# A GNN kernel: stores awaited one block later, row statistics made inside the edge count, and a head's sums taken out by two wide operations

## The reference

```
x = x + _L0_gnn_ref(_layernorm(x, axis=-1), L0_gnn_W_fc, L0_gnn_attn_l, L0_gnn_attn_r, L0_gnn_W_res, src, dst)
x = x + _L0_ffn_ref(_layernorm(x, axis=-1)[None], ...)[0]
x = x + _L1_gnn_ref(_layernorm(x, axis=-1), edge_index, edge_type_3, ...)
x = x + _L1_ffn_ref(_layernorm(x, axis=-1)[None], ...)[0]
```

```
hh = h.reshape(n, H, D)
ft = jnp.einsum('nhd,ed->nhe', hh, W_fc)
a1 = jnp.einsum('nhd,hd->nh', ft, attn_l)
a2 = jnp.einsum('nhd,hd->nh', ft, attn_r)
e = jax.nn.leaky_relu(a1[src] + a2[dst], negative_slope=NEG_SLOPE)
m = jax.ops.segment_max(e, dst, num_segments=n)
ee = jnp.exp(e - m[dst])
denom = jax.ops.segment_sum(ee, dst, num_segments=n)
alpha = ee / denom[dst]
agg = jax.ops.segment_sum(alpha[:, :, None] * ft[src], dst, num_segments=n)
res = jnp.einsum('nhd,ed->nhe', hh, W_res)
return jax.nn.relu((res + agg).reshape(n, H * D))
```

## Time and profile before

| | us |
|---|---|
| median of 3 runs | 3301.93 |
| lowest and highest | 3301.04, 3302.32 |
| the profiled execution's own time | 3298.07 |
| its span, first to last instruction | 3296.3 |
| PE busy | 2732.4 (83%) |
| DVE busy | 2093.9 (64%) |
| ACT busy | 1294.1 (39%) |
| mean granted TensorE clock | 0.891 |

### The profile page before, as it was taken

How to read it: one execution, slowest core, us unless ns; L and a number is a source line. 1 busy time by engine, 2 the same in 40 slices (tenths; PEclk the granted TensorE clock), 3 DMA queues, 4 the chain that set the end, 5 groups by cost and what they waited for, 6 DMA issues and landing times. The chain is left out here.

```text
span 3296.3 us, 35744 instructions
## 1 busy us (share of the span) xinstructions
PE 2732.4 (83%) x12628; PEld 2026.0 (61%) x12629; DVE 2093.9 (64%) x3230; ACT 1294.1 (39%) x1728; POOL 301.7 (9%) x148
## 2 busy tenths in 40 slices
PE   7867966888566966997999997997999599998869
PEld 3546962233236853555999985996888455565544
DVE  6755998999843545982889887506768760124351
ACT  1563217988410001113888872215556310013210
POOL 0000000000045851000000003300000000000002
PEclk9987558999868988998999997998999699999969
DMA  1556526101026545424532313425334310000031
GB/s 65 149 157 156 163 86 250 47 31 47 29 59 213 190 148 197 171 80 139 153 101 82 100 52 134 163 76 174 123 121 145 124 37 29 29 30 1 1 85 47
DMA packets 173005, 344.95 MB, mean 105 GB/s; under 512 B 28821, under 2 KB 94813, under 8 KB 172091
## 3 DMA queue, kind: packets, MB, share of 16 engines
q1 hardware_dynamic: 127924, 253.57, 25.2%
q10 hardware_dynamic: 35968, 73.97, 6.3%
q0 software_dynamic: 8960, 15.41, 1.9%
HBM read 259.93 MB, written 82.91 MB: 104 GB/s over the span
## 5 line engine op out<-in xcount | busy, mean ns | idle before, releaser
L1260 PE MATMUL rg1a_acc<-rg1a_values,rg1a_high 125*125 125x193 f32 x2400 | 407.5, 334 | 40.3 <-DMA rg1a_values<-values_dram 20.2
L1260 PEld LDWEIGHTS rg1a_acc<-rg1a_values,rg1a_high 125*125 125x125 f32 x2400 | 403.0, 192 | 45.0 <-issue 22.6
L1421 PE MATMUL gat_acc<-far_u,gat_ft 125*65 125x512 f32 x720 | 287.4, 540 | 76.2 <-DVE far_u L1485 75.8
L1302 DVE TENSOR_TENSOR rg1a_high<-rg1a_high,rg1a_lowb 125x625 f32<-125x625 f32 x240 | 194.3, 810 | 118.6 <-ACT rg1a_lowb L1278 103.6
L1421 PEld LDWEIGHTS gat_acc<-far_u,gat_ft 125*65 125x65 f32 x720 | 94.3, 142 | 265.6 <-issue 171.0
L1056 PE MATMUL rg_out<-rg_w,rg_hT 128*125 128x384 f32 x720 | 234.3, 489 | 0.0
L1942 PE MATMUL rg2a_acc<-rg2a_value_part,rg2a_wts_part 125*125 125x512 f32 x600 | 206.3, 344 | 28.5 <-DVE rg2a_wts_part L1661 18.9
L1277 ACT ACTIVATE rg1a_high<-rg1a_rows,rg_ks 125x625 f32<-125x625 f32 x240 | 196.3, 818 | 70.2 <-PE rg1a_acc L1260 40.6
L1943 PE MATMUL rg2a_acc<-rg2a_value_part,rg2a_wts_part 125*125 125x512 f32 x600 | 206.8, 345 | 0.0
L1944 PE MATMUL rg2a_acc<-rg2a_value_part,rg2a_wts_part 125*125 125x512 f32 x600 | 205.2, 342 | 0.0
L1056 PEld LDWEIGHTS rg_out<-rg_w,rg_hT 128*125 128x125 f32 x720 | 135.7, 189 | 97.5 <-issue 1.8
(11 more groups left out here) (433 smaller groups left out, 5205.0 us busy)
## 6 DMA issues: line engine op xcount, KB each, us to landing
rg2a_values<-values_dram SPq DMA_DIRECT2D x90, 384.0 KB, 3.3
rg1a_values<-values_dram SPq DMA_DIRECT2D x240, 96.0 KB, 1.9
rg_mask<-far_dram SPq DMA_DIRECT2D x60, 312.5 KB, 3.4
moe_raw<-in_L_ffn_w SPq DMA_DIRECT2D x16, 1152.0 KB, 6.8
gat_rows<-rows_dram SPq DMA_DIRECT2D x12, 1250.0 KB, 5.7
rg1a_rows<-shift_dram SPq DMA_DIRECT2D x24, 625.0 KB, 6.8
relw_chunk<-in_L_gnn_W ACTq DMA_DIRECT2D x36, 384.0 KB, 3.1
sorted_dram<-gat_zeros SPq DMA_DIRECT2D x30, 384.0 KB, 10.9
```

Of the source, the lines that this page charges most:

```text
L1260: last = pe.matmul(tile_of(u, d), wts[i % HB][:, d * TP:(d + 1) * TP], stream[i % 4][:, :], start=first and d % per_bank == 0, stop=final, ...
L1302: dve.tensor_tensor(high[i % HB][:, 0:w], high[i % HB][:, 0:w], lowb[i % LB][:, 0:w], op=ALU.max).then_inc(max_done, 1)
L1421: last = pe.matmul(acc[h % 2][0:WIDTH, b, 0:c1 - c0], ft[:, t, h, :], wts[i % HB][:, c0:c1], start=(t == 0), stop=(t == NT - 1))
```

## The change

Three edits, all in the first layer.

1. SP no longer waits for the stores of `far` and `counts` in the count's block. The buffers and semaphores of these stores move into an object of their own, `CountStores`, at the other end of the on-chip memory. The waits (`wait_all`) are made by SP in the block of the first norm, and the memory is given back after it.
2. The first norm gets `stats=g.row_stats`. The ten row statistics are made by DVE in the count, one tile (two instructions) at the end of the iterations 14, 15, 17, 18, 20, 21, 23, 24, 26 and 27, with one more wait for x ahead of the first. Those are the iterations that have no merge.
3. In `take_out` the ten operations of 64 columns become two of 640. One multiplies the sums in PSUM by the reciprocals (each read 64 times) into a new buffer `shares`, tied by `link`; the other adds it to `res`.

```diff
@@ count_edges
-        far = [sb(f"far{b}", [TP, N], BF16) for b in range(2)]
-        counts = [sb(f"counts{i}", [TP, NT, GROUP], U16) for i in range(2)]
+        far, counts, far_out, counts_out = stores.far, stores.counts, stores.far_out, stores.counts_out
...
             send_counts(KT // 3 - 1)
             sp.wait_ge(x_in, 48)
-            for i in range(2):
-                sp.wait_ge(far_out[i], KT // 2 * 32)
-            for i in range(2):
-                sp.wait_ge(counts_out[i], KT // 6 * 32)
...
                 if k % 3 == 1 and k >= 7:
                     merge(k // 3 - 2)
+                elif k % 3 != 1 and k >= 14:
+
+                    t = (k - 14) - (k - 13) // 3
+                    if t == 0:
+                        dve.wait_ge(x_in, 48)
+                    if t < NT:
+                        last = row_stats(dve, g, g.x, t)
+                        if t == NT - 1:
+                            last.then_inc(stats_done, 1)
             dve.wait_ge(merged, MERGED)
+            dve.wait_ge(stats_done, 1)
@@ new, ahead of count_edges
+class CountStores:
+    def __init__(self, s):
+        self.far = [s.sb(f"far{b}", [TP, N], BF16, side="right") for b in range(2)]
+        self.counts = [s.sb(f"counts{i}", [TP, NT, 3 * TP], U16, side="right") for i in range(2)]
+        self.far_out, self.counts_out = s.sems("far_out", 2), s.sems("counts_out", 2)
+
+    def wait_all(self, sp):
+        for i in range(2):
+            sp.wait_ge(self.far_out[i], KT // 2 * 32)
+        for i in range(2):
+            sp.wait_ge(self.counts_out[i], KT // 6 * 32)
@@ normalize, at the end of SP's part
+            if stored:
+                stored.wait_all(sp)
@@ attend_narrow, take_out
-                for d in range(NT):
-                    at = slice(h * DV, (h + 1) * DV)
-                    last = dve.scalar_tensor_tensor(out=res[:, d, at], in0=by_tile[:, d // HALF, d % HALF, 0:DV],
-                                                    scalar=recip[:, d:d + 1], in1=res[:, d, at],
-                                                    op0=ALU.mult, op1=ALU.add)
-                last.then_inc(taken, 1)
+                link(dve.tensor_tensor(shares[:, :, :].rearrange("p (a d) w -> p a d w", a=2), by_tile[:, :, :, 0:DV],
+                                       recip[:, :].rearrange("p (a d) -> p a d", a=2).unsqueeze(3)
+                                       .to_broadcast([TP, 2, HALF, DV]), op=ALU.mult))
+                at = slice(h * DV, (h + 1) * DV)
+                dve.tensor_tensor(res[:, :, at], res[:, :, at], shares[:, :, :], op=ALU.add).then_inc(taken, 1)
@@ gat_layer
-                normalize(g, "gat_ln", g.x, res, hT)
+                normalize(g, "gat_ln", g.x, res, hT, stats=g.row_stats, stored=stores)
+                stored.close()
```

More of the change, by code:

```diff
@@ L53, in __init__, with sb @@
             g.semaphores_used = 0
-    def sb(self, name, shape, dt=F32):
-        return self.ctx.enter_context(self.nc.sbuf_tensor(name, shape, dt))
+    def sb(self, name, shape, dt=F32, side="left"):
+        return self.ctx.enter_context(self.nc.sbuf_tensor(name, shape, dt, side=side))
     def ps(self, name, shape):
@@ L112, in _, with count_edges @@
             pool.wait_ge(ident_done, 1)
-def count_edges(g, x, src, dst, etype):
+class CountStores:
[8 more added lines that the diff above has]
+            sp.wait_ge(self.counts_out[i], KT // 6 * 32)
+def count_edges(g, x, src, dst, etype, stores):
     with ExitStack() as ctx:
@@ L164, in count_edges @@
         far_done = sem("far_done")
-        far_out = [sem(f"far_out{b}") for b in range(2)]
         turned_done = sem("turned_done")
         turned_copied = sem("turned_copied")
-        counts_out = [sem(f"counts_out{i}") for i in range(2)]
+        stats_done = sem("count_stats_done")
         masks_in = [sem(f"masks_in{i}") for i in range(2)]
@@ L421, in turn_tile, with normalize @@
     last.then_inc(tiled, 1)
-def normalize(g, tag, src, dst, dstT, gamma=None, beta=None, eps=1e-5, beside=None, stats=None):
+def normalize(g, tag, src, dst, dstT, gamma=None, beta=None, eps=1e-5, beside=None, stats=None, stored=None):
     with ExitStack() as ctx:
@@ L1381, in attend_narrow @@
         recip = s.sb(f"{tag}_recip", [TP, NT])
+        shares = s.sb(f"{tag}_shares", [TP, NT, DV])
         acc = [s.ps(f"{tag}_acc{i}", [128, 3, 512]) for i in range(2)]
@@ L1705, in gat_layer @@
     H, DH = 12, 64
-    with ExitStack() as ctx:
-        count_edges(g, x, src, dst, etype)
+    stored = ExitStack()
+    stores = CountStores(Scope(g, stored))
+    count_edges(g, x, src, dst, etype, stores)
     with ExitStack() as ctx:
```

## The result

| | before | after |
|---|---|---|
| median, us | 3302.23 (5 runs) | 3279.46 (5 runs) |
| lowest and highest, us | 3301.04, 3304.97 | 3274.26, 3284.73 |
| the profiled execution's own time, us | 3298.07 | 3279.46 |
| its span, us | 3296.3 | 3277.7 |
| its mean granted TensorE clock | 0.891 | 0.895 |

The ratio of after to before is 0.9933, with a 95% interval of 0.9921 to 0.9945: 22.8 us less by the medians. From profile to profile it is 18.6 us less, where the sum said 17.8. The median lies 0.5 us under the low end of the range of the forecast.

A forecast was written before the change was run, and what follows sets the result against it. No engine was taken to bound the whole; each place was read for the wait that ends last. Terms 4.9 + 9.3 - 0.5 + 4.1 = 17.8 us less gave 3284.1 us against the median of 3301.93, range 3280 to 3293.

The forecast's parts named there:

- The stores' wait: End of the count's block: without SP's wait for the last stores the norm starts earlier, 4.9 us less.
- the rival that its end drains them: Count's block end: leaving it waits for the stores anyway, so the 4.9 us stay; 3289.0 us, chance 5%.
- the last rival: Statistics cost PE their full time and the block's end still waits for stores; 3297.8 us together, chance 2%.
- The statistics in the norm: Start of the first norm: DVE's 20 statistics instructions, alone on the path, go; 9.3 us less.
- The statistics in the count: Count: the same 20 instructions return, 0.93 us a tile at ten places, mostly hidden; 0.5 us more.
- the walk: Count, place by place from timelines: PE feels four of ten delays, by 0.1 to 0.2 us each; 0.5 us more.
- The lower bound of -2 us: Statistics in the count: shifted work could spare two slow PE batches of 1.0 us from clock falls.
- the statistics show in full: Count: each 0.93 us is handed on to PE, costing 9.3 for 0.5; 3292.9 us, chance 13%.
- slower: Count: PE's clock falls at each of the ten places, costing 29.3 us; 3312.9 us, chance 3%.
- The wide operations: Attention, a head's sums: two operations of 640 columns for ten, 0.34 us less a head, 4.1 us for twelve.
- The rival of dear operations: Attention: PSUM pattern and repeated operand make the wide operations dear, bringing only 1.0 us; 3287.2 us, chance 5%.
- What else could move: PE's clock in the norm, up to 0.8 us gain but nothing taken; projection, some 2 us either way allowed.

The follow-up runs named there:

- e1: The kernel before with only the stores' wait moved into the norm's block: median 3295.53 us, ratio to before 0.9993.
- e3: The kernel before with only a head's ten operations made two wide ones: median 3296.43 us, ratio to before 0.9989.
- e2: The kernel before with only the row statistics moved into the count: median 3292.60 us, ratio to before 0.9981.
- e4: The changed kernel, unaltered, timed once more: median 3282.10 us, ratio to before 0.9947.
- e7: The changed kernel with the projection's six weight loads issued by SP in the norm: median 3277.28 us, ratio to before 0.9917.
- e8: The changed kernel with the projection's weights, last two masks and first tile of counts loaded in the norm: median 3272.67 us, ratio to before 0.9908.
- e9: The changed kernel, unaltered, on one chip with e10 and e11: median 3284.13 us, ratio to before 0.9947.
- e10: The changed kernel with weights, two masks and first counts tile loaded in the norm, run again: median 3275.64 us, ratio to before 0.9917.
- e11: As e10, plus 13 unused identity matmuls keeping PE busy in the norm and projection: median 3267.71 us, ratio to before 0.9904.
- e5: The changed kernel with six extra unused statistics instructions at each of the ten places, run once: span 3301.2 us, count's last closing matmul 19.1 us later.
- e6: The changed kernel with the same statistics put behind the count's merges, run once: span 3301.1 us, count's last closing matmul 14.0 us later.

## Why the prediction held, and which terms were off

**The stores' wait: right.** The sum took 4.9 us. The start moved from 5.5 us behind SP's last issue to 0.75, so 4.8 us, in after as in e1. The 0.6 us that I took for the block's end were 0.75. The block can be left with its stores under way; the rival that its end drains them, at 3289.0, is refuted by this row, and with it the last rival, 3297.8. The cover was there too: the wait ends near 237.2 and the projection starts at 248.9.

**The statistics in the norm: right.** 9.3 us went, as the earlier trace rows had it.

**The statistics in the count: the size was off, and the walk's reasons only partly held.** I took +0.5 us. From iteration 13's closing matmul to the last one the three traces without them took 83.23 us (before), 81.94 (e1) and 83.28 (e3), mean 82.8. The eight with them in that place took 82.89 (after), 82.33 (e2), 82.63 (e4), 82.53 (e7), 82.68 (e8), 82.43 (e9), 84.63 (e10) and 82.19 (e11), mean 82.8 too. Nothing can be seen of them within the 2.4 us by which like kernels differ. Part of that difference goes with PE's clock, which was granted in full but for a fall between 160 and 170 us, or between 205 and 215, in some traces (0.83 there). With no fall the stretch took 81.94 us without the statistics and 82.19 with them; with one fall 83.28 and 82.33 to 82.89; with two 83.23 and 84.63. The walk through iteration 15 is borne out (DVE, then PE, of after; the row at 203.61 in the earlier trace rows is iteration 25's, as the prediction has it, and not 24's):

```profile
149.00 1.02 DVE L622 BATCH_NORM_STATS2 row_stats<-x_all 125x6 f32<-125x384 f32 x2
149.93 0.54 DVE L299 TENSOR_SCALAR src_hot<-number,srcT 125x1250 bf16<-125x1250 uint16 x1
```

```profile
150.68 1.36 PE L365 MATMUL sums<-src_hot,key_hot 125*125 125x512 bf16 x6 [0.47 <-DVE key_hot L300]
151.88 1.05 PE L379 MATMUL turned<-ident,cnt 125*125 125x125 f32 x8
...
161.60 1.36 PE L365 MATMUL sums<-src_hot,key_hot 125*125 125x512 bf16 x6 [1.11 <-DVE key_hot L300]
```

PE begins this batch 0.48 us later than in the earlier trace rows, and the next turning at the same time: ACT's copy had been the later of the two. Where I was wrong is the fall of the clock at 161.75, which I read as the price of a wait of 1.11 us. After the change the wait there is the same 1.11 us and the batch takes 1.36 us, at the full clock. Eleven traces have this wait at this place, all but e5 and e6. In nine the batch is fast, with and without the statistics; it is slow in before (2.23 us) and in e10 (2.29). Two more waits of 1.11 us in the trace of before, ahead of 144.54 and 193.49, had batches of 1.41 and 1.36 us. So the wait alone isn't the price. The other fall, near 208 us, stands behind a wait of 1.77 to 2.54 us in all eleven traces, and it is missing in e1 and e11 alone. The lower bound of -2 us, drawn from such falls, was the right one to have: a slow batch costs about the 1.0 us that I set for it, and the falls differ between executions of like kernels. The rivals *the statistics show in full*, with 3292.9, and *slower*, with 3312.9, are refuted at this place. e6 shows that the second is a real mechanism at another: 14.0 us, with waits of near 3 us and slow batches behind them. PE's wait for the one-hot matrices, said to come out at 11 to 13 us, was 12.5:

```profile
PE sums L365 <- DVE key_hot L300: 12.5, 19, 2.5
DVE src_hot L299 <- PE sums L365: 8.8, 9, 2.4
PE turned L379 <- ACT cnt L432: 8.1, 10, 1.9
DVE far_u L306 <- DMA masks<-far_dram: 7.1, 3, 3.0
```

And DVE's wait for PE fell from 13.1 to 8.8 us: this is about half of the idle time that the statistics used.

**The wide operations: right.** 0.82 us each and 1.60 us to the next, for 1.59 in the sum. Twelve heads give 12 x (1.93 - 1.60) = 4.0 for 4.1; the attention was 3.8 us shorter, 373.2 for 377.0. In all traces it took 377.0 to 378.1 with the ten operations and 371.5 to 373.3 with the two. Reading from PSUM added nothing: both groups have 825 ns. The rival of dear operations, 3287.2, is refuted.

```profile
L1502 DVE TENSOR_TENSOR gat_res<-gat_res,gat_shares 125x640 f32<-125x640 f32 x12 | 9.9, 825 | 0.4
L1498 DVE TENSOR_TENSOR gat_shares<-gat_back,gat_recip 125x640 f32<-125x640 f32 x12 | 9.9, 825 | 0.4
```

L1498 reads PSUM and the repeated operand, L1502 reads SBUF alone. The table of cycles in the Trainium skill's "VectorE: DVE Perf Modes", section "The TRN2 errata", which I weighed against the rows, gives 792 and 727 ns for the two, and the measurement decides against it. The formula that the same section gives for float32 `tensor_tensor`, columns plus 151 at 0.96 GHz, makes 824 ns by that page, and the trace agrees with it: 825.

**What else could move: off, and it is where most of the error is.** I took nothing for PE's clock in the norm, with a chance to gain 0.8 us, since PE would now stand for 6 us and not 20. It stood for 5.9 us and still was granted 0.50 until past 242 us; the norm took 15.4 us for 14.7, so 0.7 the other way. But e9, the same kernel, took 14.7 as well, so this is no price of the change. For the projection I allowed 2 us either way. After gave back 0.6, but e1 gave back 4.8, with a second stretch at 0.50 as told above. A shorter wait ahead of a block didn't make its PE fast, and in e11's one trace work on PE went with a norm at 0.90.

**Behind the touched blocks: not in the sum at all.** 2.3 us of the 18.6 came there, and e4, the same kernel as after, took 7.6 us more than after in these blocks (3284.3 - 873.5 for 3277.7 - 874.5). A stretch of a block that no part of the change touches, from 3112 us on, shows how. The windows over it, of after, of before and of e4:

```profile
3112.20:3128.00 15.80, 14.26 (x72) 11.98 (x71) 15.28 (x26) 0.00 (x0) 0.00 (x0) 1.00 0.00 0
```

```profile
3125.50:3148.50 23.00, 22.95 (x72) 22.44 (x71) 15.98 (x26) 0.00 (x0) 0.00 (x0) 0.50 0.00 0
```

```profile
3112.70:3136.00 23.30, 23.04 (x72) 22.53 (x71) 16.25 (x26) 0.00 (x0) 0.00 (x0) 0.50 0.00 0
```

The same 72 matmuls and 26 operations of DVE take 15.8 us at the full clock and 23.0 or 23.3 at half of it, and the changed kernel has shown both. PE's last wait ahead of the stretch, for DVE, is 2.03 us in all three. This stretch alone is worth 7.2 us, and others move the other way: the stage ahead of it took 374.7 us in after and 368.9 in before. So the agreement of 18.6 with 17.8 is closer than the reasons behind it deserve: 16.3 us were made up to the end of the attention, and the other 2.3 are luck: no edit reaches the blocks behind, and e4 shows how far they move by themselves.

**The range.** Its low end, 3280, was worked out from three runs that agreed within 1.3 us, and it held nothing for the spread of single runs. With more of them the kernel before spread over 17.8 us (29 runs) and the changed one over 10.5 (5 runs), 15.7 and 13.0 (6 runs each). The step that failed is that one: over the chips the medians of the same kernel lie 4.7 us apart, 3300.46 to 3305.16 before and 3279.46 to 3284.13 after. The other two comparisons of the changed kernel gave 18.4 and 17.7 us by medians, beside the first one's 22.8, and ratios of 0.9947, where the forecast has 3284.1 / 3301.93 = 0.9946.

## What to carry to other kernels

Look for work that stands alone behind a block's end and needs only what was there long before: it is free where another engine's ring leaves its own engine idle, if it is put between two steps in which that engine is ahead. Put behind a step that already makes PE wait, the same instructions cost 14.0 us, more than their own length of 9.3. A wait for a store belongs where its buffers or its data are next needed, and the queue that holds it is then free to load for the next block, which here was worth half as much again as the change, by the medians.

## What the runs showed of the hardware

- One and the same stretch of a kernel can run at either of the two clocks from one execution to the next, with the same instructions: 15.8 or 23.0 us in the stretch above, behind the same wait of 2.03 us, and 57 or 61.7 us in the projection. In the slow case PE was busy for 22.95 of the 23.0 us and kept 0.50 throughout. Several such blocks could make the spread of 10 to 18 us between single runs; that they are its whole cause wasn't shown. The Trainium skill calls the warm-up run-variable too, in "TensorE: Matmul & The Clock Gate", section "Part 1: The HAM clock gate", and the traces agree. It puts the loss below 1% of a span, and the 7.2 us here are 0.2% of this one, yet as large as a part of the change.
- At one place in the count a wait of 1.11 us for DVE was followed by a slow batch in two traces (2.23 and 2.29 us) and by a fast one in nine (1.36 us). One such row is no evidence that the wait costs the clock. A wait of 2.46 us in the trace of after had a fast batch behind it and only then a turning of 1.85 and a batch of 2.12 us; the fall shows behind the work that follows, not only in it. In e6 five of six waits of 2.2 to 3.2 us had slow batches (1.92 to 2.34 us) right behind them; the sixth, of 2.36 us, had a fast one (1.36).
- A block can be left while its stores are under way, at 0.75 us from the last issue to the next block's first instruction.
